# Two-layer attention and expert kernel: the first tile table from four pairs instead of five, slot scatters spread over the visits, and gathers two visits ahead from visit 9 on

## The reference

```python
x = x + _L0_xattn_ref(_layernorm(x), ctx, ctx, ...)   # gated attention
x = x + _L0_ffn_ref(_layernorm(x), ...)               # 16 experts choose tokens
x = x + _L1_xattn_ref(_layernorm(x), ctx)             # masked scores of ctx applied to x
x = x + _L1_ffn_ref(_layernorm(x), ...)               # each token goes to its top 2 of 8 experts

# _L1_ffn_ref
logits = x @ Wg + bg
top2_vals, top2_idx = top_k(logits, 2)
scores = softmax(top2_vals)
h = gelu(x @ W1[e] + b1[e])        # 256 -> 1024
y = h @ W2[e] + b2[e]              # 1024 -> 256
out = sum over the token's two experts of scores * y
return layer_norm(x + out) * gamma + beta
```

## Time and profile before

| | us |
|---|---|
| median of 3 runs | 1237.15 (1236.71 to 1237.38) |
| the profiled execution's own time | 1235.16 |
| its span in the trace | 1233.4 |
| TensorE busy | 1093.2 (89%) |
| VectorE busy | 911.2 (74%) |
| ScalarE busy | 783.9 (64%) |
| GpSimd busy | 638.6 (52%) |

### The profile page before, as it was taken

The page is one execution under the profiler, slowest core; times in us unless marked ns, Lnnn a source line. Parts: engine busy times, 40 slices in busy tenths (PEclk is TensorE's granted clock), DMA queues, the critical chain, the costliest instruction groups (busy, mean ns, idle before and its releaser), DMA issues.

```text
span 1233.4 us, 24094 instructions
## 1 busy us (share of the span) xinstructions
PE 1093.2 (89%) x8282; PEld 1009.3 (82%) x8282; DVE 911.2 (74%) x1992; ACT 783.9 (64%) x1617; POOL 638.6 (52%) x573
## 2 busy tenths in 40 slices
PE   3679999988978999999999886999999999999950
PEld 2567887877866888888898776999999999999940
DVE  5787887686665666666557884899878778877868
ACT  4766566644234555655556774887778778877835
POOL 2444443442344556655644776587755444554435
PEclk8779999989998999999999997999999999999985
DMA  6644431231225669666746955457876677767639
GB/s 206 220 155 159 143 139 61 103 119 61 89 90 185 154 180 275 171 154 176 202 90 192 318 175 164 117 149 163 184 172 160 192 193 193 181 181 194 185 86 208
DMA packets 142505, 201.65 MB, mean 163 GB/s; under 512 B 29072, under 2 KB 116432, under 8 KB 135344
## 3 DMA queue, kind: packets, MB, share of 16 engines
q1 hardware_dynamic: 108976, 158.94, 39.5%
q0 software_dynamic: 32320, 40.13, 18.8%
q10 hardware_dynamic: 1088, 1.05, 0.2%
HBM read 153.21 MB, written 47.05 MB: 162 GB/s over the span
## 4 chain that ended last, share of the span: by engine, by line
PE 71%; DVE 14%; ACT 4%; DMA 4%; issue 3%; POOL 3%; SPq 0%; DVEq 0%; ACTq 0%; POOLq 0%
PE pb L2193 16%; PE quad L2174 15%; PE quad L1230 14%; PE pb L1245 7%; PE quad L300 4%; PE pb L354 4%; PE pb L368 2%; PE quad L2168 2%; DVE Dm L529 2%; PE quad L2146 1%; ACT Dm L841 1%; PE pb L1214 1%; DMA x<-dACC 1%; PE pb L265 1%; DVE sm L1648 1%
## 5 line engine op out<-in xcount | busy, mean ns | idle before, releaser
L2402 POOL DMA_INDIRECT dOUT<-y,es x71 | 126.9, 1788 | 169.7 <-DVE y L2288 96.5
L2193 PE MATMUL pb<-wh,hh 128*128 128x256 f32 x568 | 163.0, 287 | 1.0 <-DVE hl L2275 1.0
L2193 PE MATMUL pb<-wh,hl 128*128 128x256 f32 x568 | 159.4, 281 | 0.0
L2193 PE MATMUL pb<-wl,hh 128*128 128x256 f32 x568 | 158.9, 280 | 0.0
L1404 POOL DMA_INDIRECT dACC<-ye,idxJ x64 | 100.5, 1570 | 97.3 <-ACT xeh L1343 46.4
L2360 ACT ACTIVATE gl<-quad,b1c 128x256 f32<-128x256 f32 (+1 forms) x312 | 124.2, 449 | 24.9 <-PE quad L2168 13.9
L2275 DVE TENSOR_TENSOR hl<-gl,hh 128x512 fp32r<-128x512 f32 (+1 forms) x156 | 98.7, 642 | 43.8 <-ACT hh L2365 43.5
L2193 PEld LDWEIGHTS pb<-wh,hh 128*128 128x128 f32 x568 | 107.4, 189 | 1.7 <-DVE hl L2275 1.2
L2174 PE MATMUL quad<-xh,wh 128*128 128x256 f32 x512 | 104.3, 285 | 3.5 <-issue 1.6
L2193 PEld LDWEIGHTS pb<-wh,hl 128*128 128x128 f32 x568 | 106.7, 188 | 0.0
L2193 PEld LDWEIGHTS pb<-wl,hh 128*128 128x128 f32 x568 | 106.7, 188 | 0.0
(11 more groups left out here) (336 smaller groups left out, 3325.4 us busy)
## 6 DMA issues: line engine op xcount, KB each, us to landing
w2r<-in_W SPq DMA_DIRECT2D x39, 1024.0 KB, 6.4
MB<-dM SPq DMA_DIRECT2D x16, 1024.0 KB, 5.6
wraw<-in_Wg SPq DMA_DIRECT2D x16, 512.0 KB, 6.7
wraw<-in_Wu SPq DMA_DIRECT2D x16, 512.0 KB, 8.1
wraw<-in_Wd SPq DMA_DIRECT2D x16, 512.0 KB, 5.4
W<-in_W SPq DMA_DIRECT2D x8, 1024.0 KB, 11.2
w1p<-in_W SPq DMA_DIRECT2D x7, 1024.0 KB, 9.8
b2c<-in_b SPq DMA_DIRECT2D x39, 128.0 KB, 3.3
```

The costliest lines, as they stand in the source:

```text
L2193: ins = pe.matmul(bank.t[:, 0:256], a_[s][:, c, 128 * tt:128 * tt + 128], b_[n % 3][:, 256 * c:256 * c + 256], start=half == 0 and m == 0, ...
L2402: g.indirect_dma_start(out=dOUT[:, :], out_offset=bass.IndirectOffsetOnAxis(ap=es[i % 6][:, tt, 1:2].bitcast(U32), axis=0), in_=y1[i % 2][ ...
```

## The change

The early table is made from four pairs and has nine tiles (`CUT, EARLY = 4, 9` for `5, 12`). The list of visits stays the same. From this follow the other edits:

- Stage 3 scatters the slots of pairs 0 to 3 and two calls of pair 4; the other 14 calls (28 DMAs) stand in stage 4, one between the first gathers and two in each visit until visit 6.
- From visit 9 on, POOL issues gather(i+2) in visit i instead of gather(i+3); SP loads `entries` two loop turns later.
- The stores of z of pairs 6 and 7 (`z_out`) stand behind the first gather on SP; the rows are zeroed before, for which ACT issues two more DMAs of 256 KB at i == 2 of its stage 3.
- PE transposes the first tile ahead of the last pair's logits, and the second tile's behind up(0, 1). `w_high(2)`, `w_low(2)`, `x_low(0)` move up. ACT waits for the stores of pairs 6 and 7 ahead of its first copy to `hh` (it used to wait for all ahead of the visits).

```diff
-        CUT, EARLY = 5, 12
+        CUT, EARLY = 4, 9
...
-                    for b in (B - 2, B - 1):
+                    for b in range(B - 4, B):
                         a.dma_start(by_chunk(dZ[rows(b), :]), zer[:, :, :]).then_inc(*pad_st.up("zer", by=16))
...
+                if j == PAIRS - 2:
+                    slots_out(g, CUT, 0)
+                    slots_out(g, CUT, 1)
...
+        NEXT_X = [1] + [0] * (VISITS - 1)
...
+            x_transposed(0)
             logits(pe, PAIRS - 1)
-            x_transposed(0)
             up(0, 0)
...
-            x_transposed(1)
...
-                    if half == 0 and i + 1 < VISITS:
+                    if half == NEXT_X[i] and i + 1 < VISITS:
                         x_transposed(i + 1)
...
+            w_high(2)
             gap_exp(a, PAIRS - 1)
-            for s in z_st:
-                a.wait_ge(*s.all())
+            a.wait_ge(*z_st[(PAIRS - 3) % 3].all())
...
+                        if m == 0:
+                            for j in (PAIRS - 2, PAIRS - 1):
+                                a.wait_ge(*z_st[j % 3].all())
...
-            late = [(i, c) for i in range(CUT, PAIRS) for c in range(4)]
+            late = [(i, c) for i in range(CUT, PAIRS) for c in range(4)][2:]
             g.wait_ge(*pad_st.all())
-            slots_out(g, *late.pop(0))
             gather(0)
             gather(1)
             slots_out(g, *late.pop(0))
             gather(2)
             for i in range(VISITS):
-                if i + 3 < VISITS:
+                if i + 3 < EARLY:
                     gather(i + 3)
-                for c in range(2 - i % 2):
+                elif EARLY <= i + 2 < VISITS:
+                    gather(i + 2)
+                for c in range(2):
...
-            z_out(sp, PAIRS - 2)
             sp.wait_ge(*sx_st[0].all())
...
-            z_out(sp, PAIRS - 1)
-            for s in x3_st:
-                sp.wait_ge(*s.all())
+            sp.wait_ge(*gz_ld[0].of(0))
+            z_out(sp, PAIRS - 2)
...
-                if i < VISITS:
+                if i < EARLY:
                     entries(i)
+                elif EARLY <= i - 2 < VISITS:
+                    entries(i - 2)
...
+                if i == 3:
+                    z_out(sp, PAIRS - 1)
+                    for s in x3_st:
+                        sp.wait_ge(*s.all())
```

More of the change, by code:

```diff
@@ L2262, in dve_stage4 @@
             w_low(1)
+            x_low(0)
             add_bias(v, PAIRS - 1)
             pick(v, PAIRS - 1)
-            x_low(0)
+            w_low(2)
             slots(v, PAIRS - 1)
@@ L2268, in dve_stage4 @@
             for n, (i, kind, half) in enumerate(UNITS):
-                if n + 2 < len(UNITS):
+                if 2 < n + 2 < len(UNITS):
                     w_low(n + 2)
```

## The result

The changed kernel takes **1376.82 us** (median of 4 runs, 1373.33 to 1381.11) against 1237.12 (1236.71 to 1237.38): ratio **1.1133**, 95% interval 1.1109 to 1.1157. I had forecast 1298, with a range of 1262 to 1350. The direction was right; the loss was more than twice the one forecast.

The account below looks back on a forecast made before the run. TensorE was taken to bound the visits, with an 8.4 us hole at the seam. From the profiled 1235.2 us, -5 (seam) + 67 (gather waits) gave 1297; with the runs' median 2.0 higher 1299, stated as 1298, range 1262 to 1350.

Parts of the forecast that it names:

- The gathers as the deciding term: Visits 9 to 38: gathers issued only two visits ahead make PE wait, 67 us in all.
- The seam: Between stages 3 and 4: an earlier first gather shrinks TensorE's 8.4 us hole; visits start 5 us earlier.
- (b): First gather at the seam: begins at 739.8 instead of 747.5, so up(0, 0) starts 7.9 us earlier.
- (c): ACT's first hh at the seam waits for pair 7's z store; visits start 5 us earlier of the 7.9.
- (a): Stage 3: two more DMAs on ACT cost 1.9 us, an idle gap is covered; together +1.1 us.
- The waits' size: From visit 9 on: 10.73 us of y step, POOL instructions and landing against 8.5; 2.2 us per full visit.
- L = 2.5: Time in us from the end of a gather's second instruction to usable data, taken between 1.2 and 3.8.
- The bound of 3.8 for L: Upper reading of the gather's landing time, from the first gather with the z stores running.
- The clock: Rival: after waits over 3 us TensorE runs a block at 1.2 GHz, 29 us on top, 1327; chance 0.18.
- Beta DMAs and slot scatters don't count: On POOL in the visits: they stand ahead of the y scatter, which waits anyway, so nothing was added.
- The rival of late entries: Nine-tile table too small: entries(9) arrive late, visit 9 waits once a few us more, 1303; chance 0.04.
- The gathers hidden anyway: Rival: y step, scatters, gather and landing fit into 8.5 us, only the seam counts, 1232; chance 0.05.

Follow-up runs that it names:

- e2: The kernel before, with one edit: from visit 12 on gather(i+2) in visit i instead of gather(i+3); 1341.69 us.
- e1: The changed kernel, but gather(9) and gather(10) issued in visit 7 and gather(i+3) in visit i from then on; 1262.2 us.
- e5: e1 with pair 6's z store back in its old place and pair 7's directly behind the landed first gather; 1248.21 us, ratio to before 1.0082.
- e6: e5 with the two added zero stores issued by SP instead of ACT; ratio to before 1.0085.
- e10: e6 with beta stores begun in visit 9, slot scatters over by visit 5 and every gather three visits ahead; 1232.91 us, ratio to before 0.9952.
- e4: The changed kernel, with each w2 load from visit 10 on held back on SP until the previous visit's gather has landed; 1337.75 us.
- e3: The changed kernel, with 16 identity matmuls on PE ahead of the wait for the gather in 17 of visits 9 to 38; 1369.05 us.
- e9: The changed kernel, with the same stage 4 slot scatters moved ahead, five pairs of them in visit 0; 1367.03 us.
- e12: e2 with SP also reading the entries of a visit two turns later, as in the changed kernel; 1358.78 us.

## Why the prediction was right and wrong

- **The gathers as the deciding term**: right. e2 has only the lead of two and loses 86 us in visits 8 to 38; e1 gives the lead back and loses 13.
- **The seam, (b) and (c)**: right to about a microsecond, counted from the end of POOL's last inverse root. Forecast for up(0, 0) 8.9 us behind it, measured 755.39 - 747.73 = 7.7; for down(0, 0) 19.3, measured 20.2; for up(1, 0) 23.9, measured 24.8. The gain of 5 was 5.3, and e5 shows what the z store's wait cost of it, 3.7 to 4.7 us. The first gather was quicker than I had it (1.95 us from its end to the transposes, for 2.5), and the z store landed in 5.6 us instead of 4.5.
- **(a), stage 3 1.1 us later**: not settled, probably too little. It was 6.6 us longer in the changed kernel's profile (89.8 against 83.2), but the same code varied by 10 us. Seven profiles with the four zero stores on ACT took 87.9 to 97.4 us, three with two of them on SP 86.2 to 87.5; the ratios of e5 and e6 show no difference. By its seam (24.9 us for 33.9) e10 should be 9 us faster than the kernel before, and its median is 4.3 faster.
- **The waits' size**: two steps failed, and this is the larger. It is the term "L = 2.5", with the later place of the entries on SP, which I brought in only for visit 9. Without the collision the sum nearly holds: e4 measured waits of 58.0 us (7.3 of them in visit 9) against the forecast 67, and e2 61.2 from visit 12 on, where the forecast has 60. There L was 1.8 to 2.0 (up to the transposes), y to scatter 1.45 (I took 1.75) and POOL's four instructions 6.9 us (6.48). That 6.9 is also what the page's means give; my 7.18 counted four gaps of 0.3 us where four instructions have three. With the collision L is 4.7 to 5.3 us where the load is issued 0.7 us before the gather's last instruction ends (nine visits), and 3.3 to 3.9 where it is issued 1.8 to 2.4 us before (seven). A full visit behind full ones waits 4.8 to 5.2 us instead of 2.2. By places of the group (the part tile and the three behind it) the forecast was 0.9, 3.3, 4.7, 0.3; e4 has 0.6, 2.3, 4.6, 0 and the changed kernel 0.7, 5.3, 6.0, 0. I had read which queue the DMAs stand in and what each costs to issue, but not at what moment SP lets the next large one go once its blocking wait is moved. The bound of 3.8 for L, from the gather beside the z stores, was before me; I chose a value near the quiet end.
- **The clock**: the second step that failed. I left it out of the sum and set it beside the forecast as a rival of 0.18 that would cost 29 us. It was no alternative but a part of it: 27 us of longer PE work in e2 and e4, 34 in the changed kernel. There each of the 17 waits of 4.8 us or more was followed by a slow `down`, 2.0 us each on average; I had twelve at 2.4. What I held against it, that the waits are shorter than the hole at the seam and stand between dense work, does not protect: a wait of 5 us was followed by a `down` at half clock, as the chain above has it. e3 shows it by experiment. That is the behaviour which the Trainium skill, page TensorE: Matmul & The Clock Gate, section HAM oscillation, describes, a loop that goes cold in each turn at its wait for data; the trace agrees, with 5.01 us for a `down` of 2.84.
- **"Beta DMAs and slot scatters don't count"**: wrong ahead of visit 9. Slot scatters overfilled POOL, and visit 9 waited 13.6 us, of which e9 gives back 7. The rival of late entries (0.04) foresaw a wait there, but of a few us and for another reason.
- **The sum.** From the forecast 1298: the waits came out 39 us longer (106 for 67), the clock added 34, which makes 1371. The remaining 6 of 1377 are the size of the doubt about stage 3. That the sum of all upper bounds in the prediction is 1377 too is chance: it had 145 us of waits and no clock, where 106 and 34 were measured. Of the 138.5 us in visits 8 to 38, some 52.6 go with the w2 loads beside the gathers (e4 against the changed kernel), 73.2 with the lead of two from visit 10 on (e1 against e4), clock included in both, and 12.7 with visit 9, which e1 still has. With the twelve-tile table SP's order alone costs 37 (e12 against e2).
- **The gathers hidden anyway** (0.05) did not come. Only the place of the group that the forecast also had near nothing has no wait, and visit 14.

## What to carry to other kernels

The distance of a prefetch also sets beside which other transfers it runs. When a buffer wait is moved on an issuing queue, ask for every large transfer behind it at which moment it will now start, and what short, urgent transfer it will then lie beside; here a gather of 256 KB with a 1 MB load beside it came 1.4 to 3.4 us later, in 16 of 29 visits.

If a sum says that TensorE will wait several microseconds in each turn of a loop, the clock is a term of that sum, not an alternative to it, as all 17 long waits of this kernel show. Take its price from a row at half clock and add it once per long wait.

An engine that idles in one stretch and is overfull in the next can be helped by moving the same work ahead (e9), and the parts of a losing change are worth running apart: the seam was good, the lead was not.

## What the runs showed of the hardware

From the end of a gather's last instruction to the transposes that waited for it, 1.8 to 2.0 us went by in e4 (visits 10 to 38, except 2.4 in visit 14), where no w2 load ran beside it. In the changed kernel it was 4.7 to 5.3 us with a 1024 KB load issued 0.7 us before that end, 3.3 to 3.9 with one issued 1.8 to 2.4 us before it, and 1.9 to 2.0 for part tiles with one issued 0.55 us after it. Why the two delay one another was not looked at further; the window 904.9 to 911.3 shows the DMA engines 0.77 busy at 223 GB/s.

TensorE at a granted clock of 0.53 behind a wait of 5.2 us ran `down` in 5.01 us, and was back at 1.00 by 898, right behind that block. 3.7 us of matmuls on the identity in the wait kept it at 1.00.

The profiles of one and the same stage 3 differed by up to 10 us (81.5, 83.2, 91.3), and those of the same seam by 7. That is larger than most effects looked for here, while the medians of 13 and 21 runs of the kernel before agree to 1.4 us. A stage should be compared over several profiles, or left to the medians.
